# The first block of the projections in four parts, in other PSUM banks, and its second-half parts made ahead

## What is computed

```python
x = x + s4_conv(attention(x, Wq, Wk, Wv, Wo, k_cache, v_cache, ...))   # 32 sequences x 32 tokens x 512
x = x + gated_lora_ffn(x @ W.T + b + lora(x), Wq2, Wk2, W2, A, Bm)
```

## Time and profile before

| what | value |
|---|---|
| runs | 1330.68, 1333.55, 1333.70 us; median 1333.55 |
| profiled execution | 1330.66 us |
| its span on the core | 1328.8 us |
| mean granted TensorE clock | 0.976 |
| PE busy | 1252.7 us (94%) |
| DVE, ACT, POOL busy | 812.1, 810.9, 768.2 us |
| first PE pass | 11.56 us |
| last product of the first half | 674.74 us, 3.70 long |

### The profile page before, as it was taken

The page is one execution under the profiler, slowest core; times in us unless marked ns, Lnnn a source line. Parts: engine busy times, 40 slices in busy tenths (PEclk is TensorE's granted clock), DMA queues, the critical chain, the costliest instruction groups (busy, mean ns, idle before and its releaser), DMA issues.

```text
span 1328.8 us, 28755 instructions
## 1 busy us (share of the span) xinstructions
PE 1252.7 (94%) x7378; PEld 1044.1 (79%) x7378; DVE 812.1 (61%) x1724; ACT 810.9 (61%) x2256; POOL 768.2 (58%) x901
## 2 busy tenths in 40 slices
PE   6899969999999998998989999699999999999998
PEld 4678859989999986765657788598989899978756
DVE  5976546776767666852147766376776767665412
ACT  3676658888888873431135766478888888744320
POOL 3444348888888864533033434388888888754310
PEclk9999979999999998998989999799999999999999
DMA  7241388888888825305134322888888888234200
GB/s 242 88 135 63 123 235 221 234 244 241 233 229 237 233 64 171 124 1 191 37 108 127 114 93 87 243 226 236 239 241 231 234 233 236 76 114 151 101 0 32
DMA packets 148104, 214.82 MB, mean 162 GB/s; under 512 B 25844, under 2 KB 120374, under 8 KB 142006
## 3 DMA queue, kind: packets, MB, share of 16 engines
q1 hardware_dynamic: 128646, 202.75, 52.3%
q10 hardware_dynamic: 18576, 9.05, 2.5%
q0 software_dynamic: 800, 2.10, 0.5%
HBM read 203.33 MB, written 10.49 MB: 161 GB/s over the span
## 4 chain that ended last, share of the span: by engine, by line
PE 81%; DVE 6%; issue 3%; DMA 3%; ACT 3%; ACTq 2%; POOL 1%; SPq 0%; DVEq 0%; POOLq 0%; PEldq 0%
PE PS L1031 17%; PE PS L999 9%; PE PS L930 4%; PE PS L926 4%; PE PS L922 4%; PE PS L1040 4%; PE PS L1090 3%; PE PS L1081 3%; PE PS L1087 3%; PE PS L966 2%; PE PS L968 2%; PE PS L1139 2%; PE PS L901 2%; PE PS L984 2%; PE PS L988 2%
## 5 line engine op out<-in xcount | busy, mean ns | idle before, releaser
L574 POOL TENSOR_TENSOR kv_parts<-kv,k_hi 128x544 fp32r<-128x544 f32 x192 | 258.6, 1347 | 41.7 <-ACT k_hi L765 40.2
L1031 PE MATMUL PS<-probT,kv 128*128 128x128 f32 x2048 | 270.5, 275 | 0.0
L527 POOL TENSOR_TENSOR ring_parts<-ring,kv_parts 128x512 fp32r<-128x512 f32 x96 | 128.9, 1349 | 229.8 <-ACT kv_parts L641 229.8
L1031 PEld LDWEIGHTS PS<-probT,kv 128*128 128x128 f32 x2048 | 249.0, 192 | 0.1
L1461 DVE COPY probT<-PS 128x512 f32<-128x512 f32 x256 | 175.6, 686 | 3.1 <-PE PS L999 3.1
L804 ACT ACTIVATE ring<-ring,smin 128x544 f32<-128x544 f32 x192 | 143.8, 749 | 37.8 <-DVE smin L1455 36.8
L1455 DVE CUSTOM_DVE_ANT_0 ring<-PS,mask,rq 128x544 f32<-128x544 f32 x192 | 150.1, 782 | 21.8 <-PE PS L989 13.5
L765 ACT ACTIVATE k_hi<-kv 128x544 fp32r<-128x544 f32 x192 | 126.0, 657 | 52.6 <-PE PS L989 48.7
L605 POOL TENSOR_TENSOR ring_parts<-ring,kv_parts 128x512 fp32r<-128x512 f32 x64 | 89.3, 1400 | 104.5 <-ACT kv_parts L844 104.4
L562 POOL TENSOR_SCALAR ring<-ring,rinv 128x512 f32<-128x512 f32 x192 | 133.3, 694 | 0.0
L922 PE MATMUL PS<-kv_parts 128*128 128x512 f32 x384 | 115.1, 417 | 18.4 <-ACT kv_parts L641 15.7
(11 more groups left out here) (212 smaller groups left out, 2711.2 us busy)
## 6 DMA issues: line engine op xcount, KB each, us to landing
kv<-in_kpages SPq DMA_DIRECT2D x512, 128.0 KB, 2.3
kv<-in_vpages SPq DMA_DIRECT2D x496, 128.0 KB, 3.2
ring<-in_w SPq DMA_DIRECT2D x46, 1024.0 KB, 4.9
kv<-in_xT SPq DMA_DIRECT2D x4, 1024.0 KB, 8.8
v_new<-kv ACTq DMA_DIRECT2D x64, 64.0 KB, 2.9
k_new<-kv ACTq DMA_DIRECT2D x16, 256.0 KB, 2.3
kv<-k_new SPq DMA_DIRECT2D x32, 128.0 KB, 2.6
kv<-v_new SPq DMA_DIRECT2D x32, 128.0 KB, 2.4
```

What stands on the lines that cost most here:

```text
L574: nc.gpsimd.tensor_tensor(kbuf_lo(par)[:, :, g, :], kbuf(par)[:, :, g, :], k_hi[:, e % 2, :].rearrange("p (j t) -> p j t", t=PSIZE), ALU.s ...
L1031: mm = nc.tensor.matmul(PS[:, at:at + D], vbuf(bpar)[:, c, gg * D:(gg + 1) * D], probT[:, g % 2, c * P:(c + 1) * P], start=(c == 0 and a = ...
```

## The change

x and the first weights come in four DMAs each, of 256 KB, by turns (x part 0, weights part 0, x part 1, ...), each part with a semaphore of its own. In the second half's turn SP first waits for slot 0 of the ring and then issues all eight. ACT, DVE and POOL make the parts of block 0 of the first half ahead of their loops, and those of the second half inside the first half's end: ACT after the last `z_hi`, DVE after the last `z_lo`, POOL after the lower parts of the last weights. PE takes block 0 part by part: for part c four hi passes, four x_lo passes and four w_lo passes, one for each tile, into banks 4 to 7; only the last four of the 48 passes tell `proj_ready`. The wait for `out_ready` moves from block 0 to block 1. The counts of the ring's semaphores are adapted.

```diff
-            def load_x(h):
-                sp.dma_start(xA, xT_d[:, h * HT:(h + 1) * HT].rearrange("(c p) t -> p c t", p=P))\
-                    .then_inc(x_in, 16)
-
-            load_x(0)
-            load_w(0, 0)
+            def load_first(h):
+
+                if h:
+                    sp.wait_ge(w_free, h * (BLOCKS // 2) + 1)
+                for c in range(KC):
+                    rows = slice(c * P, (c + 1) * P)
+                    sp.dma_start(xA[:, c, :], xT_d[rows, h * HT:(h + 1) * HT]).then_inc(x_in[c], 16)
+                    sp.dma_start(slot(0)[:, c, :], w_d[0, :, c * 512:(c + 1) * 512]).then_inc(w_first_in[c], 16)
+
+            load_first(0)
...
-                    load_x(1)
-                    for n in range(3):
+                    load_first(1)
+                    for n in range(1, 3):
                         load_w(1, n)
...
+            for c in range(KC):
+                lower_of(0, 0, c)
             with pool.Fori(0, HALVES) as h:
...
-                for n in range(2):
-                    for c in range(KC):
-                        lower(n, c)
+                for c in range(KC):
+                    lower(1, c)
...
+                with pool.If(h < 1):
+                    for c in range(KC):
+                        lower_of(1, 0, c)
...
+            def upper_first(h):
+
+                for c in range(KC):
+                    act.wait_ge(x_in[c], 16 * (h + 1))
+                    nc.scalar.activation(x_hi[:, c, :], xA[:, c, :], ACT.Copy).then_inc(xhi_ready, 1)
+                    act.wait_ge(w_first_in[c], 16 * (h + 1))
+                    nc.scalar.activation(block_hi[:, c, :], slot(0)[:, c, :], ACT.Copy).then_inc(bhi_ready, 1)
+
+            upper_first(0)
             with act.Fori(0, HALVES) as h:
...
-                    nc.scalar.activation(stage[:, m % 2, :], bank(m), ACT.Copy).then_inc(v_read, 1)
+                    nc.scalar.activation(stage[:, m % 2, :], bank(4 + m if col == 0 else m), ACT.Copy).then_inc(v_read, 1)
...
-                act.wait_ge(x_in, 16 * (h + 1))
-                for c in range(KC):
-                    nc.scalar.activation(x_hi[:, c, :], xA[:, c, :], ACT.Copy).then_inc(xhi_ready, 1)
-                    upper(0, c)
...
+                with act.If(h < 1):
+                    upper_first(1)
                 for m in range(TILES):
                     act.wait_ge(qk_ready, 4 * h + m + 1)
...
                         if n == 1:
-                            pe.wait_ge(v_read, h * (2 * TILES) + m + 1)
+                            pe.wait_ge(out_ready, KC * (h + 1))
...
-                pe.wait_ge(out_ready, KC * (h + 1))
-                whole_block(0)
+                for c in range(KC):
+
+                    pe.wait_ge(xhi_ready, h * KC + c + 1)
+                    pe.wait_ge(bhi_ready, h * PROJ + c + 1)
+                    for m in range(TILES):
+                        nc.tensor.matmul(bank(4 + m), x_hi[:, c, m * P:(m + 1) * P], block_hi[:, c, :],
+                                         start=(c == 0), stop=False)
+                    pe.wait_ge(xlo_ready, h * KC + c + 1)
+                    for m in range(TILES):
+                        nc.tensor.matmul(bank(4 + m), x_lo[:, c, m * P:(m + 1) * P], block_hi[:, c, :],
+                                         start=False, stop=False)
+                    pe.wait_ge(blo_ready, h * PROJ + c + 1)
+                    for m in range(TILES):
+                        mm = nc.tensor.matmul(bank(4 + m), x_hi[:, c, m * P:(m + 1) * P], slot_lo(0)[:, c, :],
+                                              start=False, stop=(c == KC - 1))
+                        if c == KC - 1:
+                            mm.then_inc(proj_ready, 1)
...
+            lower_x(0)
+            with dve.Fori(0, HALVES) as h:
...
+                with dve.If(h < 1):
+                    lower_x(1)
                 for m in range(TILES):
                     dve.wait_ge(q_read, 4 * h + m + 1)
```

More of the change, by code:

```diff
@@ L68, with w_count, w_landed @@
 NCONST = _at
+def w_count(n):
+    return 16 * (BLOCKS // SLOTS - (n % SLOTS == 0))
+def w_landed(n):
+    return 16 * (n // SLOTS + (n % SLOTS != 0))
 def constants():
@@ L276, in build @@
         space_in = sem("space_in")
-        x_in = sem("x_in")
+        x_in = [sem(f"x_in{c}") for c in range(KC)]
+        w_first_in = [sem(f"w_first_in{c}") for c in range(KC)]
         w_in = [sem(f"w_in{n}") for n in range(SLOTS)]
@@ L521, in _, with lower_of @@
         def _(pool):
+            def lower_of(h, n, c, i=0):
+                pool.wait_ge(bhi_ready, h * PROJ + i * (4 * KC) + n * KC + c + 1)
+                pool.sem_inc(pool_past, 1)
+                nc.gpsimd.tensor_tensor(slot_lo(n % SLOTS)[:, c, :], slot(n % SLOTS)[:, c, :],
+                                        block_hi[:, (n % 2) * KC + c, :], ALU.subtract)\
+                    .then_inc(blo_ready, 1)
+            for c in range(KC):
+                lower_of(0, 0, c)
             with pool.Fori(0, HALVES) as h:
                 def lower(n, c, i=0):
[L525 to L529, removed]
-                for n in range(2):
-                    for c in range(KC):
-                        lower(n, c)
+                    lower_of(h, n, c, i)
+                for c in range(KC):
+                    lower(1, c)
                 for n in range(KU):
@@ L636, in upper @@
                     if c == 0:
-                        act.wait_ge(w_in[n % SLOTS], h * (16 * BLOCKS // SLOTS) + i * 16 + 16 * (n // SLOTS + 1))
+                        act.wait_ge(w_in[n % SLOTS], h * w_count(n) + i * 16 + w_landed(n))
                         if n >= 2:
@@ L840, in _ @@
                     if a == 0:
-                        act.wait_ge(w_in[n % SLOTS], h * 96 + 16 * (4 + n // SLOTS))
+                        act.wait_ge(w_in[n % SLOTS], h * w_count(n) + w_landed(12 + n))
                     if head >= 4:
@@ L919, in whole_block @@
                                 pe.wait_ge(bhi_ready, at + c + 1)
-                            if m == 0 and n == 0:
-                                pe.wait_ge(xhi_ready, h * KC + c + 1)
                             nc.tensor.matmul(bank(m), x_hi[:, c, ms], hi[:, c, :], start=(c == 0), stop=False)
                         for c in range(KC):
-                            if m == 0 and n == 0:
-                                pe.wait_ge(xlo_ready, h * KC + c + 1)
                             nc.tensor.matmul(bank(m), x_lo[:, c, ms], hi[:, c, :], start=False, stop=False)
@@ L1110, in _ @@
                 pe.wait_ge(u_act, 2 * h + 2)
-                pe.wait_ge(w_in[0], h * 96 + 96)
+                pe.wait_ge(w_in[0], (h + 1) * w_count(0))
                 for t in range(KC):
@@ L1336, in at_roots, with lower_x @@
                 link(V.tensor_tensor(S[:, 1, 0], S[:, 1, 0], cx[:, 11], ALU.subtract))
-            with dve.Fori(0, HALVES) as h:
+            def lower_x(h):
                 for c in range(KC):
```

## The result

The changed kernel takes **1341.97 us** (median of 4 runs, 1340.65 to 1342.65) against 1332.88 for the kernel before (4 runs, 1330.68 to 1333.7), a ratio of 1.007 with a 95% interval of 1.0052 to 1.0087. It is slower by some 9 us, 0.7%; the forecast was 1335.0 in a range of 1327.5 to 1338.5, "no change". The profiled execution took 1341.36 us with a span of 1339.6, 10.8 more than the span of before, at a mean granted clock of 0.972 (0.976 before).

The account below looks back on a forecast made before the run. The prediction took ACT's value stores at each half's start as the bound. It summed +2.2 us (first half) and -0.5 (second) to +1.7, 1332.4 on the profiled 1330.66, or 1335 as a median, range 1327.5 to 1338.5.

Parts of the forecast that it names:

- What bounds the start: Start of each half: ACT's value stores, not PE's blocks 0 and 1, set when the stage ends.
- Rival A: Both halves' starts: PE's lead reaches the end, 5.8 us and 8.1 us gained, total 1319.7; chance 0.15.
- The first store starts at 21.1: First half's start: ACT's first value store begins at 21.1 against 18.96, 2.2 us later.
- ACT's table load ends at 6.90: First half's start: table load ends as before, so PE's first pass comes at 8.17, 3.4 us earlier.
- slow beginning: First half, block 0: PE's first passes run at half rate after idling, charged 2.47 us from the convolution.
- upper bound of 3.2: First half's first store: at most 3.2 us later, if the slow stretch costs 3.5 instead of 2.47.
- Four stores take as long as before: Value stores after block 0, both halves: still 2.74 us apart, so no time lost between first and fourth.
- Behind the stores: First half after the fourth store: PE idles for ACT, possible second slow start; taken as 0, upper bound 0.5.
- Change of halves: Second half's start: first pass at 679.46 (678.5 to 680.4), fourth store 0.5 us earlier; 1.5 earlier to 0.4 later.
- Moved parts 0: First half's tail: ACT's copies and DVE's and POOL's parts fit into idle time, cost 0.
- B: First 20 us: the eight part loads land late, one behind the other, total 1338.6; chance 0.09.
- C: Convolution: its `conv_kernel` load is freed by more and the slow clock goes, 3.8 us, total 1331.4; chance 0.06.

Follow-up runs that it names:

- e6: The changed kernel with SP issuing the sixteen DMAs of the first four value stores of each half, ACT only copying: 1332.34 us.
- e4: The changed kernel with the weight load set off by block 0's end issued only after block 1 (likewise block 5 in the second half): 1339.77 us.
- e2: The changed kernel with x and the first weights in one 1 MB load each, in both halves: 1343.14 us.
- e5: The kernel before, unchanged, run and profiled once more: 1329.87 us in a single run.
- e8: The changed kernel with block 0 tile by tile, and POOL starting block 2's lower parts only after DVE's eight table instructions: 1329.18 us.

## Why the prediction was wrong, point by point

- **What bounds the start: right.** The chain goes through ACT's stores, as was read from the earlier trace rows. e6 shows it: the same copies and issues, but the issues on SP, 9.6 us less, of which the load behind the stores may be 2.2 (e4). Rival A fell for the reason given: PE starts earlier in the first half (10.18 against 11.56), and DVE's first unit comes 7.5 later.
- **"The first store starts at 21.1": failed**, at its first step. "ACT's table load ends at 6.90" was taken over unchanged. The prediction counted SP's six new DMAs against SP's own queue ("0") and not against ACT, which issues at the same time; the table load ended at 8.97. That is 2.07 us; the terms behind it, 1.27 and 12.96 with 2.47 for the slow beginning, measured 1.21 and 12.73. The upper bound of 3.2 was passed by 0.75. e2 shows the step: without SP's six issues the table load ends at 6.87.
- **"Four stores take as long as before": failed**, +1.36 and +1.71. The pace of 2.74 was one copy and four issues with nothing beside them. Once the whole block ends ahead of the stores, SP's 1 MB load that it sets off (23.76 in the first half, 696.94 in the second) runs beside them: one landing took 4.54, and the third copy waited 3.27 for it. e4 gives the load 0.8 and 0.6; the rest came back as one long issue, whose reason is open.
- **"Behind the stores": failed** as a reading, +2.17. The table's 2.77 was taken from one execution in which DVE had won against POOL. By e5 and e8 this is an outcome of 2.1 us either way that the kernel before has too; a sentence in the prediction should have put it into the range.
- **Change of halves: half right.** The jump was foreseen (first pass 679.46, on the conservative side); it came 4.21 behind the last products' start, where it was 4.72, and the first store was 0.67 earlier against 0.2. But the half as a whole lost 0.75 instead of winning 0.5, by the same pace of the stores. One of the readings that gave its bounds was loose: DVE's 2.38 stands in its row as a wait for ACT, not as a jump.
- **Moved parts 0: not shown wrong** in the tail itself. Everything later was taken as shifted only, and behind the second half's start 3.4 us appeared; 1.2 of them are in attention, at DVE's `q_lo`.
- **Rivals B and C** were not it: the data were in time (PE's passes are dense from 15.4 on), and the 0.53 between PE dense and the last products, part of which C would have to be, is far from its 3.8. The 2.0 us per DMA that the prediction takes from the Trainium skill (DMA: Bandwidth & Descriptors, "Anatomy of one DMA") stand there for the path of GpSimd's DMAs; these were SP's, and the sum did not use them. The time of B was nearer than the forecast, for another reason: not the landing of parts but their issue.

With its terms as measured, the two starts give +7.16 and +0.75; the remaining 2.9 (3.42 less 0.53) lie in stages whose code is unchanged, placed in part and not explained. Without them and without the tables, which fell differently in the two executions, the marks give +5.7 where +1.7 was forecast; that is the mechanism's miss. The three missed terms came from work on another queue or engine next to the one that was followed.

## What to carry to other kernels

When a block is made part by part so that PE can start sooner, all its tiles end together; if the consumer takes them one by one at PE's own pace, the early start buys nothing and the late first tile is lost. Before moving the producer, take the issues off the consumer: alone in the kernel before this gave 2.7 us, early tiles alone gave 1.5, and the two together 9.6. A DMA issue that is added to one engine has to be costed on every engine that issues in the same microseconds.

## What the runs showed of the hardware that was not expected

- Two engines that issue DMAs at once can slow each other: beside eight loads on SP, four issues on ACT lasted 4.41 us instead of 2.05, and SP's eighth 2.08 where its second to sixth took 0.42 to 0.43; with two loads (e2) ACT's four took 2.10.
- Single issues of ACT of 0.95 to 1.55 us among others of 0.32 occur with a 1 MB load beside them (second half of the changed kernel: four issues 3.41 us) and without (e4), there as the eighth of a run of issues.
- DVE's eight table operations take 2.77 or 4.98 us in executions of one and the same kernel, by which of DVE and POOL is held up.
- Both halves' attention, whose code is the same, took 1.4 and 1.2 us longer behind the changed start, 0.8 of it at one operation of DVE that is issued 0.37 us late. Left open.
